# Gather of the first expert layer's rows on GpSimd: a wait on the down products taken out, and the fetch of row numbers put ahead of the gather

## What is computed

```python
x = x + _L0_xattn_ref(_layernorm(x), ctx_1024, ctx_1024, itok_BxS2_0_31, mask_BxS2_ff1, ...)
x = x + _L0_ffn_ref(_layernorm(x), router_w, w1, w2, expert_scale)
x = x + _L1_xattn_ref(_layernorm(x), ctx_1024, ...)
x = x + _L1_ffn_ref(_layernorm(x), Wg, bg, W1, W2, W3)

def _L0_ffn_ref(hidden_states, router_w, w1, w2, expert_scale):
    logits = xf @ router_w.T
    top_w, top_idx = jax.lax.top_k(jax.nn.softmax(logits), 2)      # 8 experts, 2 for each token
    combine = jnp.sum(one_hot(top_idx, 8) * softmax(top_w)[..., None], axis=1)
    h = jax.nn.silu(jnp.einsum('td,efd->tef', xf, w1))              # 256 -> 1024
    y = jnp.einsum('tef,edf->ted', h, w2)                           # 1024 -> 256
    return jnp.einsum('te,ted->td', combine, y * expert_scale[None, :, None])
```

## Time and profile before

| | |
|---|---|
| median of 3 runs | 1481.72 us (1477.65 to 1489.85) |
| the profiled execution, its own time | 1481.72 us |
| its span, first to last instruction | 1479.9 us |
| granted TensorE clock, mean of the core | 0.959 |
| busy PE / DVE / ACT / POOL | 1352.3 / 854.3 / 816.0 / 673.4 us |
| share of the DMA engines in the expert stage (434 to 809 us) | 0.92 |

### The profile page before, as it was taken

One profiled execution on the slowest core, in us unless ns is written; L12 is line 12 of the kernel. 1 busy time (PEld: TensorE's weight loads), 2 busy tenths in 40 slices (PEclk: granted clock), 3 DMA queues, 4 the chain that ended last, 5 costly groups with the idle time before them and its releaser, 6 DMA issues.

```text
span 1479.9 us, 37453 instructions
## 1 busy us (share of the span) xinstructions
PE 1352.3 (91%) x12922; PEld 1105.3 (75%) x12922; DVE 854.3 (58%) x2352; ACT 816.0 (55%) x1907; POOL 673.4 (46%) x936
## 2 busy tenths in 40 slices
PE   6999999998369999999998799999983999999996
PEld 5787777776236666666666699999982998888896
DVE  4777778777633223332331577777763666666664
ACT  4787777875245555554553455555542455444443
POOL 3235555554443333333330457777755344444322
PEclk8999999999689999999999899999995999999998
DMA  4333433432059999987897233332223433333331
GB/s 130 106 112 106 105 100 111 114 102 52 19 118 176 196 207 178 183 168 148 160 176 153 62 93 94 92 89 87 87 65 73 133 122 115 125 121 110 127 108 52
DMA packets 280856, 172.97 MB, mean 117 GB/s; under 512 B 212990, under 2 KB 259296, under 8 KB 280676
## 3 DMA queue, kind: packets, MB, share of 16 engines
q1 hardware_dynamic: 257940, 134.79, 38.7%
q0 software_dynamic: 18608, 32.21, 7.8%
q10 hardware_dynamic: 4128, 3.57, 1.0%
HBM read 93.44 MB, written 31.97 MB: 85 GB/s over the span
## 4 chain that ended last, share of the span: by engine, by line
PE 62%; POOL 3%; DMA 3%; issue 2%; ACT 1%; DVE 1%; SPq 0%; DVEq 0%; POOLq 0%; ACTq 0%
PE psum L2310 14%; PE psum L1347 12%; PE psum L1360 12%; PE psum L2326 7%; PE psum L1830 3%; PE psum L1911 3%; PE psum L1836 3%; PE psum L1901 2%; DMA b_hT<-b_h 1%; POOL dram_ids L1677 1%; PE psum L1880 1%; PE psum L1877 1%; ACT c_prT L1761 1%; PE psum L2294 1%; PE psum L1857 0%
## 5 line engine op out<-in xcount | busy, mean ns | idle before, releaser
L2310 PE MATMUL psum<-d_xT,d_w 128*128 128x256 f16 (+1 forms) x2304 | 229.3, 256 | 1.3 <-issue 1.3
L1347 PE MATMUL psum<-arena,b_xT 128*128 x852 | 198.9, 384 | 22.5 <-DMA b_xT<-b_x 20.9
L1278 DVE SCALAR_TENSOR_TENSOR b_h<-b_hid,b_h 128x1024 f16<-128x1024 f32 x71 | 87.0, 1225 | 227.7 <-ACT b_h L1310 222.4
L2310 PEld LDWEIGHTS psum<-d_xT,d_w 128*128 128x128 f16 x2304 | 199.5, 98 | 20.6 <-issue 1.3
L1360 PE MATMUL psum<-arena,b_hT 128*128 x1704 | 198.1, 273 | 6.4 <-DMA b_hT<-b_h 6.4
L1360 PEld LDWEIGHTS psum<-arena,b_hT 128*128 128x128 f16 x1704 | 166.1, 98 | 42.9 <-issue 10.6
L1347 PEld LDWEIGHTS psum<-arena,b_xT 128*128 128x128 f16 x852 | 84.1, 99 | 112.6 <-issue 29.3
L1188 POOL DMA_INDIRECT b_xg<-dram_normed,b_gi x71 | 69.6, 980 | 216.6 <-issue 138.9
L2370 ACT ACTIVATE d_sg<-psum 128x256 f32<-128x256 f32 (+1 forms) x192 | 66.0, 348 | 145.2 <-PE psum L2310 136.9
L2428 DVE SCALAR_TENSOR_TENSOR d_hf<-psum,d_sg 128x256 f32<-128x256 f32 (+1 forms) x192 | 71.3, 378 | 104.7 <-ACT d_sg L2370 83.7
L1305 ACT ACTIVATE b_hid<-psum 128x512 f32<-128x512 f32 x142 | 83.6, 596 | 84.0 <-PE psum L1347 76.3
(11 more groups left out here) (320 smaller groups left out, 2983.1 us busy)
## 6 DMA issues: line engine op xcount, KB each, us to landing
d_wst<-in_L_w SPq DMA_DIRECT2D x64, 384.0 KB
stage<-in_L_w SPq DMA_DIRECT2D x32, 512.0 KB
dram_expert_rows<-b_ys SPq DMA_DIRECT2D x71, 128.0 KB
ctxT<-in_ctxT SPq DMA_DIRECT2D x64, 128.0 KB
dram_normed<-xn SPq DMA_DIRECT2D x64, 128.0 KB
x<-in_x SPq DMA_DIRECT2D x32, 128.0 KB, 4.7
dram_x<-xnew SPq DMA_DIRECT2D x32, 128.0 KB
c_x<-dram_x SPq DMA_DIRECT2D x32, 128.0 KB
```

Source lines behind the costliest of these rows:

```text
L1278: dve.scalar_tensor_tensor(out=h16[:, p, 1, :], in0=hid[:, p, :], scalar=H_SCALE, in1=h16[:, p, 0, :], op0=ALU.mult, op1=ALU.subtract).the ...
L1347: i = pe.matmul(psum[:, 1 + 2 * p + half, :], xT[:, j % NT, px, c, :], weights(e, c, pw, half * 512, 512), start=(n == 0), stop=(n == len( ...
L2310: i = pe.matmul(psum[:, q, m * n:(m + 1) * n], w16[:, fc % RING, pw, col:col + P], xT[:, p, px, c, at:at + n], start=(k == 0), stop=(k == ...
```

## The change

`gather(j)` no longer waits for `down_done`; its waits for `xlo_ready` and for the row numbers stay. And in the loop `load_ids(j + 2)` is now emitted ahead of `gather(j)` instead of behind it.

```diff
                     if inside(j):
                         if due(j - NX + 1):
                             pool.wait_ge(xlo_ready, j - NX + 1)
-
-                            pool.wait_ge(down_done, j - NX + 1)
                         pool.wait_ge(i_ld[j % NX], nth(j, NX))
                         pool.indirect_dma_start(xg[:, j % NX, :], None, xs[0], bass.IndirectOffsetOnAxis(ap=gi[:, j % NX, 0:1], axis=0)
                                                 ).then_inc(g_ld[j % NX], 16)
@@
                 for j in range(N_B):
+                    load_ids(j + 2)
                     gather(j)
-                    load_ids(j + 2)
                     if j == 10:
                         clear(pool)
```

## The result

The changed kernel takes 1492.80 us in the median of 14 runs (1487.03 to 1499.34), beside 1483.28 us for 14 runs of the kernel before (1476.23 to 1489.85). The ratio is 1.0066, with a 95% interval from 1.0051 to 1.0083: slower, with medians 9.5 us apart. The forecast was 1481.5 us in a range up to 1491; the median lies above the range. The loss is inside 1%, where I had put 0.91.

What follows compares the result with a forecast made beforehand. The prediction took the expert stage to be bound by PE, with the DMA engines close behind. It summed 1481.7 + 0.6 (fetch order) + 1.1 (advanced pairs) - 1.9 (gather waits saved) = 1481.5 us, range 1474 to 1491.

Steps and rivals of the forecast that it cites:

- What bounds the kernel: Expert stage: bound by PE, busy 370.61 of 375.08 us, with the DMA engines close behind at 0.92.
- rival A: Every block: transposes come late, down products wait for hT; 1501 us, or 1520 if all reaches PE; chance 0.06.
- the cost of the advance: Fill: five gather-and-fetch pairs moved earlier delay transposes PE waits for; 1.1 us, bounds 0 and 2.7.
- The saving: Up products: five gaps behind late gathers vanish once ACT stops waiting; 1.9 us, bounds 0 and 5.4.
- ACT's gather waits: Expert stage: ACT's idle time until gathers land falls from 94.4 us to about 11, nearly all the first.
- rival C: Gaps before up products: gathers were not what was late, so only costs remain; 1483.4 us, chance 0.10.
- B: Expert stage: gather waits cost PE more than gaps show, so faster within noise; about 1476 us, chance 0.08.
- The fetch ahead of the first gather: Stage start: one more GpSimd instruction before the first gather, on PE's path in full; 0.6 us, bounds 0 and 1.25.

Runs made afterwards that it cites:

- e5: Changed kernel with down_done wait back, its lead growing one block every four, at most five; 1487.26 us, 1.0033 of the kernel before.
- e2: Kernel before with only the row-number fetch moved ahead of the gather, wait kept; 1485.26 beside 1483.16 us, 1.0015.
- e8: e5 with lead capped at 2 behind block 30, plus ten extra 8-byte fetches in a row after pair 30; 1491.81 us, 1.0080 of the kernel before.
- e10: e8 with ten memsets, each waiting for the one before, in place of the extra fetches; 1481.12 us, 1.0005 of the kernel before.
- e11: e8 with five extra fetches instead of ten, on another chip; 1459.38 us, 0.9994 of the kernel before.
- e7: Kernel before with e5's gradual lead, and gathers 4 and 5 held until up products 0 and 1 are done; 1485.28 us, 1.0029.
- e3: Changed kernel with the down_done wait kept for gathers 6 to 16, dropped from gather 17 on; 1497.15 us, 1.0093 of the kernel before.

## Why the prediction was wrong

**What bounds the kernel** was read rightly. In the steady state blocks still take 5.21 us, and a gather still goes out about 1.1 us after an up product starts (463.29 and 464.42 us), so rival A, late transposes in every block, did not happen. The idle time that came is not spread; it is in one place.

**The step that failed is the cost of the advance.** I wrote as bounds "0, if the idle engines of the fill (share 0.59) take them up, and 5 x 0.54 = 2.7 us, if each delays a transpose for which PE waits", and took 1.1. Both bounds count only the work of the DMA engines, and the upper one does not hold. Where the gathers would go was right (forecast 423.6 to 436, gathers 6 to 9 stand at 422.23, 424.94, 427.44 and 430.04; 10 and 11 waited for the stalled split and came at 439.19 and 442.07), and so was the pace of 2.5 us for a pair; but I priced the five pairs by their share of the DMA engines and did not ask what a row of 23 DMAs without a pause does to others. Measured: +11.7 us by up(4). Of these 11.7, 3.0 stand before down(0), whose transpose took from 422.26 to 429.07, 6.8 us instead of 4.45 (423.06 to 427.51); 4.6 lie in down(0), which lasted until 436.7; and 4.1 in up(3), the wait for hT(1) and down(1), of which 2.7 are the low clock (4.16 and 4.07 against 2.76 and 2.81 us). I had forecast 4.5 us for the first two waits for hT; they are 4.67 + 2.87 = 7.5.

The trace of before held a hint that I passed over: the silu at 424.93 that waited 2.85 us for an up product recorded as running without a gap. A signal late in a fill whose work is on time deserved a question.

**The saving was not seen.** ACT's gather waits went as forecast; the three that are left stand at 410.05, 412.47 and 415.05 us, all in the fill. Yet three gaps before up products remain, at 484.87, 543.79 and 775.69 us, 0.9 us in the list of waits, with no gather to wait for: the sign that the prediction had named for its rival C. And e5, where the long stall is gone too, is 4.3 us slower and not 1.9 faster. So the argument that an up product late behind a late gather is a loss that the advance returns is not borne out; rival C (the gathers were not what was late) is nearer, though its 1483.4 us lacks the stall as well, and B is excluded.

**The fetch ahead of the first gather** was priced at 0.6 us. The gather did go 0.6 us later after the first fetch (3.81 against 3.21 us), but up(0) came only 0.24 us later in one execution and 0.25 in e2's, within the bounds and not "in full"; e2's whole time, +2.1 us with an interval from -0.6 to +5.2, neither confirms nor refutes it.

**Where the rules stood.** Two sentences of the Trainium skill bear on this. In "SBUF — State Buffer", section "Who interferes with whom", it says that DMA never contends with a compute engine; in "DMA: Bandwidth & Descriptors", section "Anatomy of one DMA — SWDGE (gpsimd) path", that one can emit many descriptors before their cost shows up. By the first taken at its word, e8 would equal e10. Measured they are 11.7 and 1.1 us above the kernel before. The sentence stands in a section on the memory's ports, and no run here shows what PE waits for, so a fight for a port is not shown; but that DMAs leave TensorE alone does not hold for GpSimd's in a row, and there the measurement decides. The second speaks of what a DMA itself costs, and agrees with the issue of 0.95 us for entries of 8 bytes and of 1 KB alike, in the row too; of what a row does to other engines it says nothing.

**Still open.** Which shared thing a row fills up: nothing here looks into the queue, and PE's single steps of 0.7 us and the late signals would fit several. Whether it needs DMAs or only instructions that GpSimd starts without a wait. The length from which a row hurts, between 7 and 12 if the chip of e11 behaves like the others, and whether a short pause resets it fully. And the 4.3 us of e5 and the 2.3 of e7: e10, with the same lead until block 30 but 2 after it, equals the kernel before, which would point at a price of the full lead later in the stage; but from up(20) to up(70) the traces of e5 and e10 take 272.35 and 272.34 us, so they show no such price, and point at the blocks in which the lead grows instead. One trace each can't settle it. Last, every time on record comes with a span and a clock from a profile, so no run tells whether the stall is the same without one. No version beat the kernel before.

## What to carry to other kernels

While TensorE works, let GpSimd's DMAs meet a wait every few instructions. A wait that looks superfluous can be what paces them: here taking it out made a row of 23, and a lead won in one burst cost 9.5 us while the engine that it relieved had slack. Before a prefetch is made deeper, count how many DMAs GpSimd can then issue in a row, and how many of them fall beside matmuls; and where PE runs in single matmuls, a wait's releaser is "remote" and the DMA share is near 0, look at what GpSimd was issuing in the 10 us before.

## What the hardware did that I had not expected

- A row of 12, 16 and 23 indirect DMAs that GpSimd issued without a pause beside matmuls, one each 1.25 us, cost PE 9.3, 12.6 and 11.7 us (e8, e3, changed kernel). Its matmuls came singly, 0.71 us apart in e8, from 9 us into the row in e8 and 11 in e3 until 2 to 3 us after its end.
- Completion signals arrive late in it: ACT waited 9.22, 9.49 and 9.09 us (changed kernel, e3, e8) for matmuls long recorded as ended, and in e8 SyncE waited as long for the same signal, while GpSimd's own DMAs went on.
- Size does not make it (8-byte entries do it), a busy GpSimd does not (ten memsets, each with a wait: 1.0005). Ten DMAs spread over ten blocks did not (1.0009), on a chip where no row was seen to hurt.
- It costs a second time. With PE in single steps the granted clock fell, to a mean of 0.66 over 5 us in the changed kernel, 0.58 over 6 us in e3 and 0.50 over 5 us in e8 (552 to 557 us), and the next up product took 4.16 us in the changed kernel, part of it at the 1.2 GHz level, instead of 2.76.
